# The outer products of keys and values, cut into four quarters and placed between the four products of the gate's projection

## What is computed

```python
# x: layer-normed input, 4 x 1024 x 256; xr, xk, xv, xg: x mixed with the token before it
r, k, v = xr @ Wr.T, xk @ Wk.T, xv @ Wv.T      # 16 heads of 16 channels
g = gelu(xg @ Wg.T)                            # the gate
def step(state, inp):                          # one chunk of the sequence
    rc, kc, vc = inp
    att = rc @ kc
    yc = att * Wmat @ vc + rc @ state * wb     # within the chunk, and across from the state
    new_state = ws * state + kc * wk @ vc      # kc * wk @ vc: the outer products
    return new_state, yc
out = group_norm(y) * g @ Wo.T
```

## Time and profile before

| what | value |
|---|---|
| time, median of 3 runs | 896.36 us (894.65 to 896.64) |
| the profiled execution's own time | 896.49 us |
| its span, first to last instruction | 894.8 us |
| TensorE matmuls busy | 846.2 us, 95% of the span |
| TensorE weight loads busy | 705.4 us, 79% |
| VectorE, ScalarE, GpSimd busy | 472.9, 489.2, 467.1 us |
| mean granted TensorE clock | 0.992 |

### The profile page before, as it was taken

One profiled execution on the slowest core, in us unless ns is written; L12 is line 12 of the kernel. 1 busy time (PEld: TensorE's weight loads), 2 busy tenths in 40 slices (PEclk: granted clock), 3 DMA queues, 4 the chain that ended last, 5 costly groups with the idle time before them and its releaser, 6 DMA issues. The chain is left out here.

```text
span 894.8 us, 18307 instructions
## 1 busy us (share of the span) xinstructions
PE 846.2 (95%) x6791; PEld 705.4 (79%) x6791; DVE 472.9 (53%) x1173; ACT 489.2 (55%) x876; POOL 467.1 (52%) x497
## 2 busy tenths in 40 slices
PE   3999999999999999889999999999999999999995
PEld 2777777777777777779889889879789889889885
DVE  6788788788888766343441442442351443342430
ACT  4578787777777779263542443443452444453331
POOL 4434766777767675564337355237346137447014
PEclk9999999999999999999999999999999999999998
DMA  5852132112111121546116236025417024314013
GB/s 154 320 193 67 50 102 67 62 56 80 38 38 38 38 98 53 170 150 139 42 42 118 86 92 111 5 78 89 112 48 137 22 72 92 82 42 54 7 19 42
DMA packets 50465, 73.93 MB, mean 83 GB/s; under 512 B 5056, under 2 KB 42176, under 8 KB 50368
## 3 DMA queue, kind: packets, MB, share of 16 engines
q1 hardware_dynamic: 35488, 53.46, 18.0%
q0 software_dynamic: 14592, 19.18, 12.5%
q10 hardware_dynamic: 288, 0.01, 0.0%
HBM read 38.41 MB, written 34.22 MB: 81 GB/s over the span
## 5 line engine op out<-in xcount | busy, mean ns | idle before, releaser
L1540 POOL TENSOR_TENSOR wlo<-wraw,whi 128x448 fp32r<-128x448 f32 x84 | 107.1, 1278 | 201.5 <-ACT whi L1597 201.5
L1817 PE MATMUL p<-xh,whi 128*128 128x512 f32 (+1 forms) x504 | 190.4, 378 | 7.3 <-DVE xl L1716 4.7
L1819 PE MATMUL p<-xh,wlo 128*128 128x512 f32 (+1 forms) x504 | 189.7, 376 | 0.0
L1818 PE MATMUL p<-xl,whi 128*128 128x512 f32 (+1 forms) x504 | 189.3, 376 | 0.0
L1734 DVE TENSOR_TENSOR hid<-gated,p 128x512 f32<-128x512 f32 (+1 forms) x126 | 81.1, 644 | 204.3 <-ACT gated L1611 204.3
L1548 POOL DMA_INDIRECT out<-ysb,index x80 | 126.0, 1575 | 85.2 <-ACT ysb L1633 55.1
L1611 ACT ACTIVATE gated<-p 128x512 f32<-128x512 f32 (+1 forms) x126 | 70.8, 562 | 179.7 <-PE p L1819 179.7
L1837 PE MATMUL py<-whi,hh 128*128 128x256 f32 x469 | 135.1, 288 | 6.2 <-DVE hl L1742 3.1
L1839 PE MATMUL py<-whi,hl 128*128 128x256 f32 x469 | 132.8, 283 | 0.0
L1838 PE MATMUL py<-wlo,hh 128*128 128x256 f32 x469 | 132.5, 283 | 0.0
L1817 PEld LDWEIGHTS p<-xh,whi 128*128 128x128 f32 x504 | 94.7, 188 | 27.4 <-DVE xl L1716 5.4
(11 more groups left out here) (192 smaller groups left out, 1441.1 us busy)
## 6 DMA issues: line engine op xcount, KB each, us to landing
wraw<-in_w SPq DMA_DIRECT2D x24, 896.0 KB
disp<-wraw SPq DMA_DIRECT2D x16, 662.5 KB, 9.2
xtok<-disp SPq DMA_DIRECT2D x16, 530.0 KB, 4.5
x_ring<-in_x SPq DMA_DIRECT2D x16, 256.0 KB, 3.0
out<-x SPq DMA_DIRECT2D x16, 256.0 KB
xtok<-disp SPq DMA_DIRECT2D x8, 265.0 KB, 6.1
out<-ysb,index POOLq DMA_INDIRECT x80
disp<-row,slot_i POOLq DMA_INDIRECT x64
```

The costliest lines, as they stand in the source:

```text
L1540: nc.gpsimd.tensor_tensor(wlo[e.const % 2][m][:, cut], wraw[k][:, cut], whi[e.const % 2][m][:, cut].bitcast(F32), ALU.subtract).then_inc(w ...
L1817: nc.tensor.matmul(dst[:, 0:w], hi[m][:, wcut], xh[xcut], start=(kt == 0), stop=False)
L1818: nc.tensor.matmul(dst[:, 0:w], hi[m][:, wcut], xl[xcut], start=False, stop=False)
L1819: ins = nc.tensor.matmul(dst[:, 0:w], lo[m][:, wcut], xh[xcut], start=False, stop=(kt == KT - 1))
```

## The change

`project_g` and `outer` become one call, `project_g_and_outer`. It waits for the gate's mixed input and for `v_ready` before its first matmul, and then goes through the four matmuls of the projection. Behind each of these it puts one quarter of the outer products, the four bands of one `(t, c)`. `proj_done[3]` is signalled by the fourth matmul of the projection, ahead of the last quarter; `kv_done` by the last band. The matmuls themselves, their operands and their number are the same, as is every other engine's order.

```diff
--- before.py
+++ after.py
@@ -1182,6 +1182,29 @@
                 pe.wait_ge(mixed_ready[3], b + 1)
                 project(b, 3, pB)
 
+        def project_g_and_outer(b):
+
+            if 0 <= b < STEPS:
+                pe.wait_ge(mixed_ready[3], b + 1)
+                pe.wait_ge(v_ready, b + 1)
+                if b == 0:
+                    pe.wait_ge(proj_in[3], 16)
+                for m in range(KT):
+                    for c in range(KT):
+                        ins = nc.tensor.matmul(pB[:, m, :], w_in_sb[3][:, c, m * P:(m + 1) * P], mixed[3][:, c, :],
+                                               start=(c == 0), stop=(c == KT - 1))
+                        if m == c == KT - 1:
+                            ins.then_inc(proj_done[3], 1)
+                        ins = outer_half(m, c)
+                ins.then_inc(kv_done, 1)
+
+        def outer_half(t, c):
+            for d in range(BANDS):
+                band = slice(d * 2 * N, (d + 1) * 2 * N)
+                ins = nc.tensor.matmul(p_kv[band, t, c, :], k_dec[:, t, c * P + d * 2 * N:c * P + (d + 1) * 2 * N],
+                                       v_pad[:, t, c * BANDS + d, 0:4:3, :], start=True, stop=True)
+            return ins
+
         def turn1(b):
             if 0 <= b < STEPS:
                 pe.wait_ge(xn_ready, b + 1)
@@ -1198,17 +1221,6 @@
                     for c in range(KT):
                         ins = nc.tensor.transpose(p_k[:, t, c * P:(c + 1) * P], kT[:, c, t * Q:(t + 1) * Q], ident[:])
                 ins.then_inc(kt_done, 1)
-
-        def outer(b):
-            if 0 <= b < STEPS:
-                pe.wait_ge(v_ready, b + 1)
-                for t in range(TPS):
-                    for c in range(KT):
-                        for d in range(BANDS):
-                            band = slice(d * 2 * N, (d + 1) * 2 * N)
-                            ins = nc.tensor.matmul(p_kv[band, t, c, :], k_dec[:, t, c * P + d * 2 * N:c * P + (d + 1) * 2 * N],
-                                                   v_pad[:, t, c * BANDS + d, 0:4:3, :], start=True, stop=True)
-                ins.then_inc(kv_done, 1)
 
         def scores(b, t):
 
@@ -1337,8 +1349,7 @@
             scores_a(c)
             across(c, 0)
             turn1(c + 1)
-            project_g(c)
-            outer(c)
+            project_g_and_outer(c)
             within(c, 0, 0)
             scores_b(c)
             within(c, 0, 1)
@@ -1361,8 +1372,7 @@
 
         scores_a(15)
         across(15, 0)
-        project_g(15)
-        outer(15)
+        project_g_and_outer(15)
         within(15, 0, 0)
         scores_b(15)
         within(15, 0, 1)
```

## The result

| what | before | after |
|---|---|---|
| time, median of 4 runs | 896.50 us (894.65 to 899.32) | 907.48 us (904.88 to 910.19) |
| ratio, 95% interval | 1 | 1.011 (1.0084 to 1.0136) |
| span of the profiled execution | 894.8 us | 906.9 us |
| TensorE matmuls busy | 846.2 us | 862.1 us |
| mean granted TensorE clock | 0.992 | 0.989 |

What follows compares the result with a forecast made beforehand. TensorE bounds steps 0 to 3, a ring of ScalarE and GpSimd steps 7 to 13. Terms 3.9 + 1.2 + 0.1 + 0.6 = 5.8 us on 896.4 give 902.2 us, chance 0.73; 8-in-10 range 897.8 to 905.5.

Steps and rivals of the forecast that it cites:

- price of a round trip: On TensorE, from full to banded matmuls and back: 0.32 us; three more a step, 0.97 us.
- first rival: Passages almost free behind short quarters: 0.36 us a step, 1.4 in steps 0 to 3, 897.9 us; chance 0.11.
- the second: TensorE's stall vanishes and TensorE was the bound in steps 7 to 15: 894.4 us, faster; chance 0.06.
- the stop: TensorE's halt amid the outer products, steps 7 to 15; expected after in the third quarter, with 0.8 us left.
- Steps 0 to 6: Steps 0 to 3 all on the path, 3.9 us; steps 4 to 6, less the 0.56 us mask wait, 1.2 us.
- The ring of steps 7 to 15: ScalarE and GpSimd, through to the next four indirect DMAs, set the pace of steps 7 to 13, not TensorE.
- The cover: Steps 7 to 13: waits of 0.23 us before `project_r` and 0.6 before `decayed_r` cover a difference of 0.7.
- the third rival: The stop returns without cover before `decayed_r`: 0.6 us more in each of nine steps, 907.7 us; chance 0.10.
- Its sign: In steps 8 to 13 `decayed_r` waits for TensorE instead of mostly for ScalarE if the third rival holds.
- Steps 7 to 13: Waits cover nearly all added TensorE time: 0.1 us more for all seven steps, range 0 to 2.
- Step 14: `decayed_r` already waits 0.67 us for TensorE, so there is no cover: 0.3 us more.
- Step 15's block: Behind it TensorE goes on into the experts' products: 0.3 us more.

Runs made afterwards that it cites:

- four free comparisons: Changed kernel against kernel before in sessions at the 883 us level: unchanged, both with memsets for indirect DMAs, and twice both with `mixed_g` moved forward; 15.5 to 17.8 us more.
- r2_after: The changed kernel, unchanged, measured again beside the kernel before in a held session: 908.5 us against 900.8, ratio 1.010.
- r1_before: The kernel before, unchanged, run again for its profile: 898.4 us.
- e3_halves: Changed kernel with the outer products in two halves instead of four quarters, held session: 906.4 us, ratio 1.0066 to the kernel before.
- e4_outer_first: Changed kernel with all outer products in one piece ahead of the projection, held session: 921.0 us, ratio 1.0227 to the kernel before.
- e16_before_busy_last: Kernel before with GpSimd's four indirect DMAs a step replaced by memsets of about the same length, held session: 885.6 us against 897.2, ratio 0.9864.

## Why the forecast was too low

**The price of a round trip was right.** 0.32 us each was worked out from `within` before `project_k`; the block takes 3.10 us against 3.07, and all four free comparisons give 15.5 to 17.8 us for 16 steps. The 0.10 us at each passage and the late load of the full weights were both paid in every quarter. The first rival is out, and so is the second: the stop didn't vanish.

**Steps 0 to 6 were right.** 3.83 and 1.30 us against 3.9 and 1.2. In steps 4 to 6 `scores_b` no longer waits for the masks, save that they start 0.12 us later in step 6: the longer block covers it, as forecast. That depends on the session: in `r2_after` the block stops in steps 5 and 6 already.

**The ring of steps 7 to 15 was read rightly, but the stop was put in the wrong place.** This is the step that failed: "28 MATMUL behind `across` end in the third quarter ... with the fourth product and its quarter still to do, 0.8 us". In after, step 8 stops with 21 MATMUL behind `across` (four transposes, four of the projection, 13 outer), in the second quarter. So do all of steps 7 to 15, with 19 to 23. What stands behind the release is then 186.57 - 184.84 = 1.73 us of work, against 0.24 before, so 1.49 more. The cover that I had counted is 0.23 + 0.6 = 0.83 us. The rows of after give 0.78. `project_r` starts 1.99 us after `within` instead of 2.32, which gives 0.33. `decayed_r` starts 0.18 us after the end of `across` instead of 0.63, which gives 0.45: the signal's 0.18 us can't be covered, and I had counted them. 1.49 - 0.78 = 0.71 a step; measured over steps 7 to 14 were 4.80 / 8 = 0.60. With 0.8 us behind the release, 0.56 more than before, the cover would have held. So the cover was there (the third rival had it missing), and the work was larger than it: the rival's effect by another cause, and its number came near the result by luck. Its sign, `decayed_r` waiting for TensorE, came true and doesn't tell the two apart.

I had also compared the block's end with its start. In a ring the right measure is from the release on: before, `decayed_r` starts 188.04 - 180.01 = 8.03 us after it, in after 193.58 - 184.84 = 8.74. That difference of 0.7 is the growth of a step.

The four orders of one held session test this account. The work left is the mean time from the last release to `within` in steps 7 to 14:

| kernel (same session) | work left, us | a step of 7 to 14, us | growth | work left more than before, less the cover of 0.78 |
|---|---|---|---|---|
| before (`r1_before`) | 0.26 | 20.43 | | |
| `e3_halves` | 1.41 | 20.76 | 0.33 | 0.37 |
| `r2_after` | 1.74 | 21.09 | 0.66 | 0.70 |
| `e4_outer_first` | 3.02 | 22.49 | 2.06 | 1.98 |

The growth follows the work left behind the release to 0.1 us in each, though the number of round trips added is one, three and one. With the piece ahead part of the time left is the lower clock.

**A fixed number of instructions doesn't describe the stop.** In step 8 it came after 28 outer and other MATMUL behind `across` in the kernel before, 21 in after, 19 with halves (4 + 4 + 11) and 15 with the piece ahead (4 + 11). Within one kernel the number isn't fixed either: in the kernel before it is 22 to 30 over steps 7 to 15, and 21 to 28 in `r1_before`. What is common is that in these steps it begins in the outer products each time; in steps 9 and 14 of after a second stop stands just ahead of the third product. The Trainium skill gives TensorE a queue depth of 64 instructions ("TensorE: Matmul & The Clock Gate", table at its head). The counts here, with a weight load to each MATMUL, are 22 to 60 in all held profiles; that doesn't contradict it, but it doesn't give the place. A reading that fits all four is that supply goes on slowly while signals are held: a product at 0.216 us a MATMUL doesn't notice, outer MATMUL at some 8 ns drain what is queued. This is argued from the place of the stop and not shown by a run.

**The terms one by one.** Steps 7 to 13, put at 0.1 us (0 to 2), took 4.6 us more. Step 14 took 0.18 more, where I had taken 0.3. Step 15's block took 1.34 us more, where I had taken 0.3: it stops twice in the second quarter in after. The same error as above.

**What stays open.** What puts a session at the held or the free level, and by what way an indirect DMA of GpSimd holds TensorE's signals. In the session of `e16_before_busy_last` the DMAs' absence ended it; in free sessions they did no harm. The runs show both, and none looks deeper. Why the supply stops where it does stays open too. No version that does the whole work beat the kernel before at either level.

## What to carry to other kernels

Count the passages between full and banded matmuls before interleaving them: 0.1 us at the passage each way and 0.1 us for a full weight load that comes late make 0.32 us a round trip, more than a quarter of the outer products takes (0.07 us), so small banded work belongs in one piece beside other banded work. Where an engine is stopped until an outside event, what a reordering costs is the work left behind the stop, from the release on, less the waits that give way to it; here short instructions ran into the stop each time, and it cost least with the long ones ahead of them (0.26 us left against 3.02). An idle gap is a gain only if the work that could fill it may be issued there, and if no cheaper wait covers it.

## What was not expected of the hardware

- The same kernel has two levels 14 us apart (883 and 897 us) that last for a session. In the upper one TensorE's signals reach ScalarE 2.5 to 3.2 us late in steps 7 to 14, while GpSimd issues indirect DMAs (in step 8 the copy at 180.12 of transposes ended at 177.49); in the lower one they come at once (0.03 us) with the same DMAs.
- In the upper level a stopped TensorE goes on 0.7 to 0.9 us after the last of a step's indirect DMAs has ended, in all eight held profiles and wherever the stop falls in its order (0.69 to 0.88; in step 8 of the kernel before 180.01 - 179.30 = 0.71).
- Replacing 64 indirect DMAs of GpSimd by memsets of about the same length took 11.6 us off in the upper level (897.2 to 885.6) and nothing in the lower.
- Stops of 0.4 to 0.5 us that follow each other within 2 us (the piece ahead, step 8) were followed by a projection of 3.20 instead of 1.99 us, with a granted clock of 0.50 (1.2 GHz) from 187 to 189 us; in three of nine steps as much idle time was followed by none of this.
